# Ordering the state partitions of a recurrent stage row by row

## What is computed

```python
def _selective_scan(u, dt, A, Bm, Cm, Dp):
    dA = jnp.exp(dt[..., None] * A)
    dBu = (dt * u)[..., None] * Bm[:, :, None, :]
    def step(h, inp):
        dA_t, dBu_t, C_t = inp
        h = dA_t * h + dBu_t
        y = jnp.einsum('ben,bn->be', h, C_t)
        return (h, y)
    ...
    return y + u * Dp
```

## Time and profile before

| | |
|---|---|
| median of 3 runs | 1708.91 us (1708.18 to 1709.97) |
| the profiled execution: its own time | 1705.7 us |
| its span in the profile | 1704.0 us |
| busy in the span: PE, DVE, ACT, POOL | 1337.6, 1387.7, 1311.6, 1075.3 us |
| TensorE's granted clock, mean | 0.924 |
| DMA | 168.19 MB, 99 GB/s over the span |

### The profile page before, as it was taken

The page is one execution under the profiler, slowest core; times in us unless marked ns, Lnnn a source line. Parts: engine busy times, 40 slices in busy tenths (PEclk is TensorE's granted clock), DMA queues, the critical chain, the costliest instruction groups (busy, mean ns, idle before and its releaser), DMA issues. The chain is left out here.

```text
span 1704.0 us, 25209 instructions
## 1 busy us (share of the span) xinstructions
PE 1337.6 (78%) x7544; PEld 694.5 (41%) x7547; DVE 1387.7 (81%) x2394; ACT 1311.6 (77%) x2978; POOL 1075.3 (63%) x714
## 2 busy tenths in 40 slices
PE   6777898996677776867776877767756899899989
PEld 4554555553322222332222332222322466566543
DVE  4655788896529999999999999999998588778835
ACT  4444787884658999999999999999975788777730
POOL 2001566661048999999999999999996254444410
PEclk9999899997978889999989988999977999999979
DMA  3000000001045434455434545443440511121000
GB/s 105 2 1 2 1 2 2 1 2 26 7 174 208 178 122 173 164 210 199 165 132 165 200 167 199 174 146 147 185 150 25 185 51 51 51 99 50 1 1 25
DMA packets 70229, 168.19 MB, mean 99 GB/s; under 512 B 20420, under 2 KB 40152, under 8 KB 56664
## 3 DMA queue, kind: packets, MB, share of 16 engines
q1 hardware_dynamic: 68680, 166.17, 27.1%
q10 hardware_dynamic: 1168, 0.53, 0.1%
q0 software_dynamic: 256, 0.01, 0.0%
HBM read 131.04 MB, written 35.65 MB: 98 GB/s over the span
## 5 line engine op out<-in xcount | busy, mean ns | idle before, releaser
L1785 POOL TENSOR_TENSOR ma_hs<-ma_dtuR,ma_Bt 128x1024 f32<-128x1024 f32 x192 | 449.4, 2369 | 12.3 <-DMA ma_dtuR<-ma_dtu_d 6.9
L914 POOL TENSOR_TENSOR x_pr<-x_pr,x_rec 128x512 f32<-128x512 f32 x256 | 267.9, 1047 | 244.2 <-DVE x_rec L1203 244.2
L1162 ACT ACTIVATE x_pr<-x_sm,x_mx 128x256 f32<-128x256 f32 x512 | 255.4, 500 | 62.6 <-DVE x_mx L1194 58.8
L1868 PE MATMUL ps<-ma_hs,ma_fold 128*32 128x512 f32 x1024 | 157.7, 744 | 180.4 <-DVE ma_hs L2204 172.3
L2016 ACT ACTIVATE ps<-ma_dtR,ma_A 128x512 f32<-128x512 f32 x384 | 248.7, 680 | 48.6 <-DVE ma_hs L2204 41.4
L1793 POOL TENSOR_TENSOR ma_hs<-ma_hs,ma_Ct 128x1024 f32<-128x1024 f32 x112 | 264.2, 2370 | 22.3 <-DVE ma_hs L2198 21.9
L2198 DVE TENSOR_TENSOR_SCAN ps<-ps,ma_hs 128x1024 f32<-128x1024 f32 x112 | 255.9, 2285 | 7.9 <-ACT ps L2016 7.9
L2046 ACT ACTIVATE ma_rowB<-ma_dtuT,ma_BT 128x128 f32<-128x128 f32 x512 | 232.8, 525 | 1.3
L2198 DVE TENSOR_TENSOR_SCAN ma_hs<-ps,ma_hs 128x1024 f32<-128x1024 f32 x80 | 180.7, 2275 | 5.3 <-ACT ps L2016 5.3
L2204 DVE TENSOR_TENSOR ma_hs<-ps,ma_Ct 128x1024 f32<-128x1024 f32 x144 | 176.3, 1224 | 5.0
L990 PE MATMUL ps<-ident,x_pr 128*128 128x128 f32 x1024 | 154.2, 283 | 17.1 <-ACT x_pT L1076 12.7
(11 more groups left out here) (325 smaller groups left out, 2594.7 us busy)
## 6 DMA issues: line engine op xcount, KB each, us to landing
ma_dtuR<-ma_dtu_d SPq DMA_DIRECT2D x32, 1024.0 KB, 6.8
ma_dtR<-ma_dt_d SPq DMA_DIRECT2D x32, 1024.0 KB, 6.6
ma_Bt<-ma_bc_d SPq DMA_DIRECT2D x16, 1024.0 KB, 5.0
ma_Ct<-ma_bc_d SPq DMA_DIRECT2D x16, 1024.0 KB, 7.4
ma_dtu_d<-ma_dtu SPq DMA_DIRECT2D x32, 256.0 KB, 2.0
ma_dt_d<-ma_dt SPq DMA_DIRECT2D x32, 256.0 KB, 2.3
keys_d<-ma_kv SPq DMA_DIRECT2D x32, 256.0 KB, 2.6
values_d<-ma_kv SPq DMA_DIRECT2D x32, 256.0 KB, 2.0
```

The lines of the kernel that those rows point to most:

```text
L914: pool.tensor_tensor(pr[:, r, :, :], pr[:, r, :, :], rec[:, r, :].unsqueeze(2).broadcast_to([P, 2, L]), ALU.mult).then_inc(pr_done, 1)
L1162: a = act.activation(pr[:, n % RP, t, :], sm[:, n % 2, t, :], ACT.Exp, bias=mx[:, n % 2, t:t + 1], scale=-1.0, accum_out=den[:, n % RP, t: ...
L1785: pool.tensor_tensor(hs[:, k % SLOTS, :, :], dtuR[:, h, q, :].unsqueeze(1).broadcast_to([P, 2, CH]), rows(Bt, k), ALU.mult).then_inc(dbu_d ...
L1868: mm = pe.matmul(c.ps[q * E32:(q + 1) * E32, Y[h], :], fold[:, :], hs[:, (k0 + q) % SLOTS, a, :], start=False, stop=(j % 2 == 1 and a == 1 ...
```

## The change

The partition becomes 32 ni + e in place of 4 e + ni. All that holds the order moves with it: the source patterns of the rates A, of Bt, Ct, dtuR and dtR; the fold matrix, now built by four affine selects; the layout of `rowB`; and dtuT, which `copy_dtu` now writes in the order (q e), so that a scaled copy reads 32 adjacent words per q and writes 32 adjacent words. The number and the order of the instructions on PE, DVE, ACT and SP stay as they are.

```diff
@@ RecurrentWeights.load
                 sp.dma_start(self.A[:, b, h, q, :],
-                             g["m_al"][i].rearrange("(h e q) (n o) -> h q e n o", h=2, q=gq, o=4)[h, q]).then_inc(done, 16)
+                             g["m_al"][i].rearrange("(h e q) (n o) -> h q n e o", h=2, q=gq, o=4)[h, q]).then_inc(done, 16)
@@ mamba_stage
-        rowB = s.sb("rowB", [P, 4, 2, GQ, E32, NI])
+        rowB = s.sb("rowB", [P, 4, 2, GQ, NI, E32])
@@ SP: Bt and Ct
-                                     bc_d[d, k * NS:(k + 1) * NS, :].rearrange("(a n o) t -> a n (o t)", a=1, o=NO)
-                                     .broadcast_to([E32, NI, NO * CH])).then_inc(done, 16)
+                                     bc_d[d, k * NS:(k + 1) * NS, :].rearrange("(n a o) t -> n a (o t)", a=1, o=NO)
+                                     .broadcast_to([NI, E32, NO * CH])).then_inc(done, 16)
@@ SP: spread, for dtuR and dtR
-                                     src[d, h].rearrange("(e a q) t -> e a (q t)", a=1, q=GQ)
-                                     .broadcast_to([E32, NI, GQ * CH])).then_inc(done, 16)
+                                     src[d, h].rearrange("(a e q) t -> a e (q t)", a=1, q=GQ)
+                                     .broadcast_to([NI, E32, GQ * CH])).then_inc(done, 16)
@@ POOL: fold
-                pool.memset(fold[:, :], 1.0).then_inc(consts, 1)
+                pool.memset(fold[:, :], 0.0).then_inc(consts, 1)
...
-                pool.wait_ge(consts, 3)
-                pool.affine_select(out=fold[:, :], in_=fold[:, :], compare_op=ALU.is_ge, fill=0.0,
-                                   base=0, pattern=[[-NI, E32]], channel_multiplier=1).then_inc(consts, 1)
-                pool.wait_ge(consts, 4)
-                pool.affine_select(out=fold[:, :], in_=fold[:, :], compare_op=ALU.is_ge, fill=0.0,
-                                   base=NI - 1, pattern=[[NI, E32]], channel_multiplier=-1).then_inc(consts, 1)
+                for ni in range(NI):
+                    pool.wait_ge(consts, 3 + ni)
+                    pool.affine_select(out=fold[:, :], in_=fold[:, :], compare_op=ALU.not_equal, fill=1.0,
+                                       base=-E32 * ni, pattern=[[-1, E32]], channel_multiplier=1).then_inc(consts, 1)
@@ PE
-                                              rowB[:, t, a, q, :, :].rearrange("p e n -> p (e n)"), c.ident[:, :])
+                                              rowB[:, t, a, q, :, :].rearrange("p n e -> p (n e)"), c.ident[:, :])
...
-                pe.wait_ge(consts, 5)
+                pe.wait_ge(consts, 3 + NI)
@@ ACT: copy_dtu
-                    act.activation(dtuT[:, :, :].rearrange("p t e -> p (t e)"), c.ps[:, PB, :], ACT.Copy).then_inc(dtuT_done, 1)
+                    act.activation(dtuT[:, :, :].rearrange("p t (q e) -> p t q e", q=GQ),
+                                   c.ps[:, PB, :].rearrange("p (t e q) -> p t q e", t=4, q=GQ), ACT.Copy).then_inc(dtuT_done, 1)
@@ ACT: scale_rows
-                    act.activation(rowB[:, t, a, :, :, ni], dtuT[:, t, :].rearrange("p (e q) -> p q e", q=GQ), ACT.Copy,
+                    act.activation(rowB[:, t, a, :, ni, :], dtuT[:, t, :].rearrange("p (q e) -> p q e", q=GQ), ACT.Copy,
                                    scale=BT[:, f % 2, t, a, ni:ni + 1]).then_inc(rows_done, 1)
```

## The result

| | kernel before | with the change |
|---|---|---|
| median | 1709.44 us (1708.18 to 1710.71, 4 runs) | 2229.47 us (2222.89 to 2256.67, 4 runs) |
| span of the profiled execution | 1704.0 us | 2222.3 us |
| TensorE's granted clock, mean | 0.924 | 0.833 |

The ratio is 1.3029 [1.2979, 1.3079]: 520 us slower. The highest of the four runs with the change, 2256.67 us, was a slow one, and the ratio leaves it out.

The account below looks back on a forecast made before the run. DVE, then POOL and ACT, nearly full in the recurrent stage; with the change, spreads on four DMA engines decide. 1705.7 + 29.5 + 15 x 17.6 + 10 = 2009 us, 2013 in the median's measure; range 1970 to 2900.

Parts of the forecast that it names:

- The division along the outermost source step: Spread transfers from HBM: four outermost source steps give only four of 16 DMA engines work, 32 pieces each.
- the copies: Scaled copies on ACT (L2046), 32 a step: 525 ns falls to 382, 4.6 us of ACT less a step.
- the copy of dtu: ACT's copy of the turned dtu (L2037), now reading PSUM in four-word steps: 0.2 us a step.
- the fold matrix: Two more affine selects on POOL at the stage's start: covered by a wait, without that cover 0.6 us once.
- two cases that were set as alternatives: Four engines at row rate (0.42, 1970 to 2065 us), or four in each other's way (0.40, 2470 to 2900 us).
- the likeliest: Four DMA engines at row rate: steps of 68 us, about 125 GB/s, 2013 us, range 1970 to 2065; chance 0.42.
- the spread term: Six 1 MB transfers a step from HBM (Bt, Ct, two dtuR, two dtR): 9.7 us each on four engines.
- the predicted chain of 68.5: Recurrent step from one landing of dtR half 0 to the next: 68.5 us instead of 50.9, 17.6 more.
- The third rival: Four engines also hinder each other: transfers 14.6 to 19.4 us, steps 98 to 126, kernel 2470 to 2900 us; chance 0.40.
- the first step: Before the first recurrent step, Bt, Ct, dtuR and dtR land later on four engines: 29.5 us once.
- the loads: Weight loads of three steps, on the same queue between dtR half 1 and Bt: 3 us each, some 10 in all.
- The first rival: All 16 engines still work, ACT's relief returns 14 us of DVE's waits: 1695 us, range 1683 to 1705; chance 0.13.

Follow-up runs that it names:

- experiment 3: Kernel before with only the source patterns of the transfers changed, copies and fold matrix as before: 2231.54 us, ratio 1.3062.
- h2: Loads-only kernel, 1 MB transfer with source pattern 2 copies x 64, to partitions 0 to 63 and 64 to 127: 54 GB/s at share 0.13.
- p2: Loads-only kernel, 0.5 MB transfer with source pattern 2 copies x 32, to partitions 0 to 63: 17.8 us, 30 GB/s at share 0.12.
- experiment 8: Two kernels: the changed one with rates A in the old order, 2224.47 us; the one before with A in the new order, 1705.89 us.
- experiment 4: The change with source patterns of the transfers put back as before, copies and fold matrix as changed: 1704.26 us, ratio 0.9974.
- t8: Loads-only kernel, 1 MB transfer with source pattern 8 copies x 16: 11.1 us at a share of 0.5.

## Why the prediction was right or wrong

**Right.** The division along the outermost source step, the choice that no row of the trace before showed, held: share 0.30, forecast 0.2 to 0.3. So did the place of the new wait (the first decay of a step, for dtR), the copies (390 ns for 382), their worth under that cover (nothing clear of noise: with them 2229, without them 2232), and the copy of dtu (no change, for 0.2 us). For the fold matrix no run stands by itself; nothing of the loss is left for it, since the old one in experiment 3 gave the same time.

**Luck: the range.** It runs from 1970 to 2900 because it spans two cases that were set as alternatives, and the time fell into the gap between them, where no case had put it. Its signs fell there too: 106 GB/s, where one case had 125 and the other under 100; ordinary steps of 80.3 us, where they had 68 and 98 or more; DVE 0.60 busy, where the likeliest had 0.7.

**Wrong: the size of the spread term.** The step that failed is "I take 9.7 us" for every transfer. It is right for a transfer behind another (9.8). The first of each train takes about 15.8 us of data: 17.8 us waited, less the 2 us that a plain transfer's 4.35 us holds beside its 2.4. Twice a step a train starts, with Bt after the store of B and C and with dtuR after the stores of dt: 2 x 6 = 12 us on the predicted chain of 68.5 makes 80.5, and the step shown took 79.7. Its three stretches bear this out: 21.1 us to Bt's issue where the chain has 22, 30.0 from there to dtuR's where it has 24.5 (46.5 - 22), and 28.6 to the next decay where it has 22. Before Bt the engines had a pause (the row from 740 us has a share of 0.13), and before dtuR SP waits for the stores to land. The rates, 61 GB/s at the train's start and 132 later in it (that stretch holds some kv stores too), say the same. The third rival was right that four engines can run below the row rate, and was too high (98 us a step or more) because it had that for the whole of every transfer. Its 14.6 us are 9.7 times the 1.5 between the two stores' rates in the earlier trace rows; the factor of 2 behind its 19.4 us, and so behind the 2900, no run shows. What the runs showed is h2's rate per engine over p2's, 26 / 16 = 1.6, some 15.8 us of data for the first of a train and 9.8 for each behind it. The truth lay between it and the likeliest case.

**Wrong: the first step and the loads.** The first decay came at 547.2 us, 48.6 later where 29.5 was foreseen. Of the 19 us between, 3.3 were there before Bt was issued; Bt with Ct took 29.9 us until dtuR was issued, some 6 more than foreseen, which is the start of a train again; and dtuR with dtR took 31.5 us for some 22, because the rate rose later than within a step (70 GB/s from 517.5 to 535 us). The loads cost 33 us where the sum had 10: SP came to the next store 13 to 14 us late (experiment 8).

In sum, against the 303.5 us foreseen: first step +19, fifteen steps +177 (15 x (80.3 - 68.5)), loads +23, the rest of the program -4, together 215; measured 518.3 - 303.5 = 214.8.

**The first rival** (16 engines, 1695 us, range 1683 to 1705) got its own run in experiment 4: 1704, at the edge of that range. Its failing step is that DVE's 13.6 us of waits for turned rows and decays would come back when ACT gets 4.6 us a step. Those waits stayed, and the relief went into ACT's waiting for DVE.

**Open.** Why four engines start at 61 to 66 GB/s, a little over half of the 106 to which they rise in a train, and why eight engines with shares of 16 partitions (t8) stayed at 109 GB/s after 123. Why dtuR and dtR before the first step speed up later than those within a step was not tried.

## What to carry to other kernels

Before a layout is changed for an engine's sake, write out the pattern of every transfer that has to follow it, and look at its outermost step: the same bytes in the same 8 KB pieces moved four to six times slower (106 and 66 GB/s for 418) because four steps stood outermost instead of 32. Ask also which partitions the engines write at the same time: two with 0 to 31 and 32 to 63 moved 16 GB/s each, two with 0 to 63 and 64 to 127 26. And where another engine is near its bound, a faster copy gives little: here 18 to 28% less of ACT's time for 512 copies was worth 0.2 to 0.3%, and the adjacent reads alone, with the old partitions, give most of it without touching a transfer.

## What was not expected of the hardware

- Transfers on few engines aren't of one speed: alone, a 1 MB transfer on four of them takes 17.8 us, and those behind it add 9.8 each.
- SP's issue of a transfer, mostly 0.3 to 0.6 us before, lasts 2.4 to 8.9 us in the rows shown while earlier, slow transfers are still being moved, so SP itself becomes late. Why it lasts longer was not tried.
- ACT reads PSUM in steps of four words at no cost (574 ns against 575), while the same step in an SBUF read costs 84 ns of 455 in a 128x128 copy.
- TensorE's clock fell to 0.76 in the stage, from 0.91, as its pauses for the other engines grew (busy for 73% of the fifteen steps before, for 53% now), and the same matmuls were busy for 1429.7 us instead of 1337.6. That delays nothing that the transfers wait for: the x rows are ready 16.0 us after a step's first decay (at 739.4), for 17.3 before.
